# A two-layer vision tower on one core: first token weights from the unturned routing, weight loads split in six pieces, later weights rounded in small steps

## The chip, the core and the metric

The kernel runs on one core of one Trainium2 chip. Its engines are TensorE (PE in the profile; PEld is its weight load), VectorE (DVE), ScalarE (ACT), GpSimd (POOL) and SyncE (SP, which here only issues DMAs). Each runs its own list of instructions in order and waits on semaphores for the others. The metric is the time of one execution on the device in microseconds (us), the median of several; less is better. The profile is of one execution, with its own time.

## What is computed

Eight images of 256x256 become 8 x 64 patch tokens of 192 features, plus one class token each: 520 tokens. Then come attention 0, expert layer 0, attention 1 (with 8-bit fake quantisation) and expert layer 1, each after a layernorm and added to the running sum. The change touches the two expert layers, and the preparation of attention 1's weights:

```python
# expert layer 0: 8 experts of 768 hidden units, best 2 a token
router_probs = softmax(x @ w_gate);  top_p, top_i = top_k(router_probs, 2);  top_p /= sum(top_p)
h = gelu(x @ w_fc[expert]);  o = (h @ w_proj[expert]) weighted by top_p and summed
# expert layer 1: 16 experts of width 128 (8) and 256 (8), best 8 a token
probs = softmax(x @ router_w.T);  comb = normalised top-8 weights, zero elsewhere
out = sum over e of comb[:, e:e + 1] * (gelu(x @ w1[:, e]) @ w2[e])
# attention 1, weights (w_qkv and w_proj)
scale = max(max(abs(w), axis=1) / 127, 1e-8);  q = clip(round(w / scale), -128, 127);  w = q * scale
```

## The kernel before

The program is one block with a hand-written list for each engine. Tokens are kept as columns in the expert layers: 520 columns, in two halves of 260 (HALF). Every product there is made of parts rounded to a shorter format, hi and lo (x = hi + lo), so that three or more products of parts replace one in f32.

**ffn(y)** is expert layer y on each engine (PE L622 ff., ACT L1024 ff., DVE L1350 ff.). It runs over tiles of 128 hidden units: 48 in layer 0 (six an expert), 24 in layer 1. On PE, `entry("h", x)` makes the hidden units of tile x, five matmuls a half; `project(x)` multiplies them by the second weights and adds to the sums in banks 2 to 5 (SUMS), five matmuls a half (L601, L660). PE runs entry x + 2 ahead of project x. On ACT, `entry` reads the bank with gelu into hid, `hi_part(x)` rounds the weighted hidden units to hid_hi (L1043). On DVE, L1363 multiplies hid by the tile's token weights (128 equal rows, tok_w), and L1368 makes hid_lo. ENTRIES is the order in which entries take the two pairs of banks; an entry waits until ACT has emptied the bank of two entries before.

**Token weights.** `route` on DVE ends in comb, tokens by experts. `comb_turn` on PE turns it (L611) into banks 2 and 3, ACT copies it to comb_t (L1068, L1069), experts by tokens. For the first expert (MADE: turn 0 in layer 0, turns 0 and 1 in layer 1) `entry("w", turn)` multiplies comb_t by a one-hot matrix row_pick (L636) to get 128 equal rows, which ACT copies to tok_w (L1034). All later experts' rows are written by SP to DRAM (comb_to_dram) and read back to all partitions (token_weights, tok_w_in).

**Weights.** A load is one expert of layer 0 (2 x 768 columns of fc, 6 tiles x 192 of pj) or four tiles of layer 1; there are 8 + 6, in two slots. SP fetches it raw, when the split of the load two before is done (w_lo_done). While the tiles of load n run, load n + 1 is split: ACT copies a piece rounded (`weights_hi`, L1019, L1021), DVE subtracts (`weights_lo`, L1344, L1347). In before a load is three pieces, handled after the tiles j = 0, 1, 2 of the running load: fc part 0, fc part 1, pj. `next_weights(x)` stands on ACT after hi_part(x), and DVE's piece after hid_lo of tile x; each engine's next tile waits behind it.

**Later weights.** `whole_weights(piece)` on DVE prepares attention 1's eight rows of 192 x 96 weights: maxima, scale, reciprocal, product, rounding by adding and taking away MAGIC, clip. Its eight pieces stand after the tiles j = 3, 4, 5 of loads 0 to 2. `turn_weights` on PE turns them after ffn(0), and ACT copies them out (L1009 ff.).

`fill(n)` issues n matmuls of zeros. `then(...)` on DVE waits for the instruction's own completion, `settle(...)` only counts it.

## Time and profile before

| | us |
|---|---|
| median of 3 runs (lowest to highest) | 341.9 (341.59 to 342.23) |
| the profiled execution | 344.13 |
| its span, first to last instruction | 342.3 |
| PE busy (matmuls) | 290.1 |
| DVE busy | 258.6 |
| ACT busy | 207.2 |
| mean granted TensorE clock | 0.939 of full |

Expert layer 0 lasts from about 45.5 to 173, expert layer 1 from 269.8 to 333. So the two take more than half of the span. A busy share is an average over stages; what ends a wait last in a stage is read from the timelines, where `[0.63 <-ACT pj_parts L1021]` means that the engine was idle 0.63 us before this row and that ACT's instruction of line 1021 released it. Matmuls are pipelined: one of 260 columns shows 0.28 us, but the next starts 0.12 us after it.

### The profile page before, as it was taken

The page shows a single profiled execution, that of the slowest core. Times are in us where ns is not written, and L with a number is a line of the kernel's source. Part 1 is how long each engine was busy: PE and PEld are TensorE (multiplying, and loading weights), DVE is VectorE, ACT ScalarE, POOL GpSimd, SP SyncE. Part 2 cuts the span into 40 slices and gives each one's busy share as a digit, 9 for nine tenths or more (in the row PEclk, how much of TensorE's full clock was granted, in tenths as well). Part 3 has the DMA queues.
Part 4 walks back from the last instruction along what each step waited for, and adds up shares of the span by engine and source line. Part 5 has one row for each costly group of instructions (what it writes and reads, how often), then busy time and mean ns, then how long its engine had stood idle before and what let it go on. Part 6 is the DMA issues. An engine that isn't in the chain of part 4 may idle for free.

```text
span 342.3 us, 6186 instructions
## 1 busy us (share of the span) xinstructions
PE 290.1 (85%) x2351; PEld 263.4 (77%) x2351; DVE 258.6 (76%) x719; ACT 207.2 (61%) x489; POOL 14.2 (4%) x39
## 2 busy tenths in 40 slices
PE   8999989898989999999978307199877889999991
PEld 7979658898988999999967205068655479999991
DVE  1355767879888888889766899889858679888851
ACT  1063466575666867768738498687032777777750
POOL 0530000000000000000010001400000000000000
PEclk9999989999999999999999855589899999999997
DMA  7980016415050531200000000002400035542401
GB/s 249 317 265 1 2 19 234 166 33 190 5 192 2 192 113 53 107 3 0 2 0 2 0 2 2 0 0 67 149 3 0 0 99 171 159 156 90 96 0 47
DMA packets 10572, 27.28 MB, mean 80 GB/s; under 512 B 1368, under 2 KB 2216, under 8 KB 10544
## 3 DMA queue, kind: packets, MB, share of 16 engines
q1 hardware_dynamic: 10096, 26.20, 23.3%
q0 software_dynamic: 448, 0.70, 0.7%
q8 instruction: 18, 0.29, 0.4%
q14 instruction: 10, 0.08, 0.1%
HBM read 26.44 MB, written 0.45 MB: 79 GB/s over the span
## 4 chain that ended last, share of the span: by engine, by line
PE 50%; DVE 31%; ACT 12%; issue 4%; DMA 1%; DVEq 0%; ACTq 0%
PE bank L601 21%; PE bank L660 7%; PE bank L581 5%; ACT hid_hi L1043 4%; PE bank L699 4%; PE bank L645 3%; PE bank L643 3%; DVE hidden_area L1363 3%; DVE fc_lo L1344 2%; PE bank L571 2%; ACT fc_hi L1019 2%; DVE hid_lo L1368 2%; DVE pj_parts L1347 2%; ACT pj_parts L1021 1%; DVE bn L1264 1%
## 5 line engine op out<-in xcount | busy, mean ns | idle before, releaser
L1043 ACT ACTIVATE hid_hi<-hidden_area 128x260 fp32r<-128x260 f32 x144 | 55.6, 422 | 45.5 <-DVE hidden_area L1363 44.5
L601 PE MATMUL bank<-hid_hi,pj_parts 128*128 128x260 f32 x288 | 76.9, 288 | 4.9 <-DVE hid_lo L1368 4.9
L1368 DVE TENSOR_TENSOR hid_lo<-hidden_area,hid_hi 128x260 fp32r<-128x260 f32 x144 | 56.3, 427 | 10.1 <-ACT hid_hi L1043 1.1
L601 PEld LDWEIGHTS bank<-hid_hi,pj_parts 128*128 128x128 f32 x288 | 54.1, 188 | 6.7 <-DVE hid_lo L1368 6.0
L1036 ACT ACTIVATE hidden_area<-bank 128x260 f32<-128x260 f32 x144 | 48.3, 376 | 5.8 <-PE bank L645 5.3
L601 PE MATMUL bank<-xt_hi,fc_hi 128*128 128x260 f32 x144 | 41.9, 291 | 1.6 <-ACT hidden_area L1034 1.3
L645 PE MATMUL bank<-xt_lo,fc_lo 128*128 128x260 f32 x144 | 41.6, 289 | 0.0
L571 PE MATMUL bank<-zeros 128*128 128x260 bf16 x239 | 34.2, 296 | 8.6 <-ACT hidden_area L1175 6.7
L601 PE MATMUL bank<-xt_lo,fc_hi 128*128 128x260 f32 x144 | 40.9, 284 | 0.0
L643 PE MATMUL bank<-xt_lo,fc_hi 128*128 128x260 f32 x144 | 40.9, 284 | 0.0
L601 PE MATMUL bank<-xt_hi,fc_lo 128*128 128x260 f32 x144 | 40.8, 283 | 0.0
L660 PE MATMUL bank<-hid_hi,pj_parts 128*128 128x260 f32 x144 | 40.7, 283 | 0.0
L601 PE MATMUL bank<-hid_lo,pj_parts 128*128 128x260 f32 x144 | 40.7, 282 | 0.0
L660 PE MATMUL bank<-hid_lo,pj_parts 128*128 128x260 f32 x144 | 40.7, 282 | 0.0
L571 PEld LDWEIGHTS bank<-zeros 128*128 128x128 bf16 x239 | 23.9, 105 | 15.0 <-issue 8.3
L1363 DVE TENSOR_TENSOR hidden_area<-hidden_area 128x260 f32<-128x260 f32 x72 | 27.8, 423 | 7.0 <-ACT hidden_area L1034 6.2
L1363 DVE TENSOR_TENSOR hidden_area<-hidden_area,xn 128x260 f32<-128x260 f32 x72 | 28.0, 424 | 2.0 <-ACT hidden_area L1036 1.8
L1344 DVE TENSOR_TENSOR fc_lo<-raw_area,fc_hi 128x768 fp32r<-128x768 f32 (+1 forms) x28 | 23.6, 844 | 7.7 <-ACT fc_hi L1019 6.5
L601 PEld LDWEIGHTS bank<-xt_hi,fc_hi 128*128 128x128 f32 x144 | 27.4, 190 | 2.0 <-ACT hidden_area L1034 1.5
L601 PEld LDWEIGHTS bank<-xt_lo,fc_hi 128*128 128x128 f32 x144 | 27.4, 191 | 0.1
L601 PEld LDWEIGHTS bank<-xt_hi,fc_lo 128*128 128x128 f32 x144 | 27.4, 190 | 0.0
L645 PEld LDWEIGHTS bank<-xt_lo,fc_lo 128*128 128x128 f32 x144 | 27.3, 190 | 0.0
(296 smaller groups left out, 545.7 us busy)
## 6 DMA issues: line engine op xcount, KB each, us to landing
raw_area<-fc_dram SPq DMA_DIRECT2D x8, 768.0 KB, 4.4
raw_area<-pj_dram SPq DMA_DIRECT2D x8, 576.0 KB, 5.4
xn<-comb_dram SPq DMA_DIRECT2D x12, 260.0 KB, 3.2
raw_area<-fc_dram SPq DMA_DIRECT2D x6, 512.0 KB, 4.0
embed_area<-embed_in_dram SPq DMA_DIRECT2D x8, 352.0 KB, 6.1
hidden_area<-comb_dram SPq DMA_DIRECT2D x9, 260.0 KB, 3.2
raw_area<-pj_dram SPq DMA_DIRECT2D x6, 384.0 KB, 4.3
score_area<-w_l_dram SPq DMA_DIRECT2D x1, 576.0 KB, 8.9
```

What stands on the lines that cost most here:

```text
L571: pe.matmul(PB[bank][:, 0:HALF], zeros[:, 0:128], zeros[:], start=True, stop=True, skip_group_check=True)
L581: last = pe.matmul(out, lhs(kc), rhs(kc), start=(kc == 0), stop=(kc == KC - 1))
L601: mm = pe.matmul(out, lhs[a], rhs[b], start=start and n == 0, stop=stop and n == 2, skip_group_check=True)
L643: pe.matmul(out, fc_hi[:, s, 1, cols], x_mix[:, tok], start=False, stop=False, skip_group_check=True)
L645: mm = pe.matmul(out, fc_lo[:, s, 1, cols], x_mix[:, tok], start=False, stop=True, skip_group_check=True)
L660: mm = pe.matmul(PB[SUMS[2 + n]][:, 0:HALF], pj_tails[:, s, j], hidden[:, x % 3, tok], start=x == 0 and part == 0, stop=part == 1, skip_gr ...
L699: return pe.matmul(PB[i][:, 0:D], patches[:, k, i * 128:(i + 1) * 128], w_tok[:, k, :], start=(k == 0), stop=(k == TOKK - 1), skip_group_c ...
L1036: act.activation(hid[:, x % 2, tok], src, ACT.Gelu_apprx_tanh).then_inc(entry_out[y], 1)
L1043: act.activation(hid_hi[:, x % 3, tok], hid_w[:, x % 2, tok], ACT.Copy).then_inc(hid_hi_ready[y], 1)
L1344: dve.tensor_tensor(lo, raw, hi.bitcast(F32), ALU.subtract).then_inc(w_lo_done[s], 1)
L1363: dve.tensor_tensor(hid_w[:, x % 2, tok], hid[:, x % 2, tok], tok_w[tile.weights][:, tok], ALU.mult).then_inc(weighted[y], 1)
L1368: dve.tensor_tensor(hid_lo[:, x % 3, tok], hid_w[:, x % 2, tok], hid_hi[:, x % 3, tok].bitcast(F32), ALU.subtract).then_inc(hid_lo_ready[y ...
```

## The change

1. The first expert's token weights come from comb itself. `weights(out, turn, n)` multiplies a column of comb, repeated 128 times, by the identity, over the blocks of 128 tokens that a half touches: three matmuls a half. Turn 0 leaves ENTRIES, is written to banks 4 and 5, and ACT copies it (`first_weights`). comb_turn comes after it, and project(0) waits for comb_t_ready. Entry 1 comes right after entry 0, then five fills. In layer 1 turn 1 stands behind entry 2, not ahead of it. row_pick, its DMA, and the zeroing of comb_t go.
2. `pieces(load)`: six pieces for a load of layer 0 (four of fc with 384 columns, two of pj with three tiles), four for one of layer 1 (two of fc with 512, two of pj with two tiles), one after each of the first tiles. The pieces of load 0 are all made during attention 0.
3. `whole_weights` has 18 pieces after the tiles j = 0 to 3 of loads 1 to 4 and two of load 5 (WHOLE_AT). MAGIC is taken away by ACT when it copies the turned weights.

```diff
         for tiles in TILES:
-            order = [("h", 0), ("h", 1), ("w", 0)]
+            order = [("h", 0), ("h", 1)]
             for x in range(2, len(tiles)):
-                order += [("w", tiles[x].turn)] * (tiles[x].first and tiles[x].made) + [("h", x)]
+                order += [("h", x)] + [("w", tiles[x].turn)] * (tiles[x].first and tiles[x].made)
...
+        def pieces(load):
+
+            if LOAD_TILES[load] == T0:
+                return [("fc", 0, 0, 3), ("fc", 0, 3, 6), ("fc", 1, 0, 3), ("fc", 1, 3, 6), ("pj", None, 0, 3), ("pj", None, 3, 6)]
+            return [("fc", 0, 0, 4), ("fc", 1, 0, 4), ("pj", None, 0, 2), ("pj", None, 2, 4)]
...
+        WHOLE_AT = [(load, j) for load in range(1, 5) for j in range(4)] + [(5, 0), (5, 1)]
...
             def load0(n):
-                sp.wait_ge(w_lo_done[n % 2], 4 * (n // 2))
+                sp.wait_ge(w_lo_done[n % 2], split_lo(n - 2))
...
+                def weights(out, turn, n):
+
+                    e = tiles[first_tile(y, turn)].expert
+                    for i in (0, 1, 2) if n == 0 else (2, 3, 4):
+                        lo, hi = max(n * HALF, i * 128), min((n + 1) * HALF, i * 128 + rows(i))
+                        mm = pe.matmul(out[:, lo - n * HALF:hi - n * HALF],
+                                       (comb0, comb1)[y][0:rows(i), i, e:e + 1].broadcast_to([rows(i), 128]),
+                                       ident[0:rows(i), lo - i * 128:hi - i * 128], start=True, stop=True)
+                    return mm
...
                 def project(x):
                     s, j = tiles[x].slot, tiles[x].j
+                    if x == 0:
+                        pe.wait_ge(comb_t_ready, 2 * (y + 1))
...
                 entry("h", 0)
+                entry("h", 1)
+                fill(5, SUMS[0])
+                pe.wait_ge(comb_ready, y + 1)
+                for n in range(2):
+                    weights(PB[SUMS[2 + n]], 0, n).then_inc(first_w_mm, 1)
                 comb_turn(y, n_exp)
-                entry("h", 1)
-                pe.wait_ge(comb_t_ready, 2 * (y + 1))
-                entry("w", 0)
...
                     j, load = tiles[x].j, tiles[x].load
-                    if j <= 2 and load + 1 < LOADS:
-                        if j == 2 and load > E0 * y:
+                    if load + 1 < LOADS and j < len(pieces(load + 1)):
+                        if j == entry_pieces(load + 1) and load > E0 * y:
                             act.wait_ge(pj_mm[y], tiles_to(y, load - 1))
                         weights_hi(load + 1, j)
...
                 entry("h", 0)
+                first_weights()
+                hi_part(0)
                 comb_turned(y, (E0, E1)[y])
                 entry("h", 1)
-                entry("w", 0)
-                for x in range(len(tiles)):
-                    if x >= 2:
-                        for e in entries_of(y, x):
-                            entry(*e)
+                next_weights(0)
+                hi_part(1)
+                next_weights(1)
+                for x in range(2, len(tiles)):
+                    entry("h", x)
+                    if ("w", tiles[x].turn) in ENTRIES[y] and tiles[x].first:
+                        entry("w", tiles[x].turn)
                     hi_part(x)
                     next_weights(x)
...
+                    k = piece - 10
+                    then(dve.tensor_scalar(wq_int[:, k], wq_raw[:, k], wq_inv[:, k:k + 1], 127.0, ALU.mult, ALU.min))
+                    dve.tensor_scalar(wq_int[:, k], wq_int[:, k], -128.0, MAGIC, ALU.max, ALU.add).then_inc(wint_ready, 1)
```

How the instructions stand now at the places that the text below speaks of. PE at the start of ffn(0), before: after entry 0 the turning of comb (L611), entry 1, and the one-hot product (L636); comb is the routing, ident the identity.

```order
L645 MATMUL bank<-xt_lo,fc_lo 128x260
L611 MATMUL bank<-ident,comb 8x128 [waits comb_ready]
L611 MATMUL bank<-ident,comb 8x128 x3
L611 MATMUL bank<-ident,comb 8x8
L601 MATMUL bank<-xt_hi,fc_hi 128x260
```

The same place after, from the end of entry 1 on.

```order
L674 MATMUL bank<-xt_lo,fc_lo 128x260
L592 MATMUL bank<-zeros 128x260 x5
L652 MATMUL bank<-ident,comb 128x128 [waits comb_ready]
L652 MATMUL bank<-ident,comb 128x128
L652 MATMUL bank<-ident,comb 128x4
L652 MATMUL bank<-ident,comb 128x124
L652 MATMUL bank<-ident,comb 128x128
L652 MATMUL bank<-ident,comb 128x8
L632 MATMUL bank<-ident,comb 8x128 [waits comb_ready]
```

Entry 1 now stands ahead of all that waits for comb, and the turning behind the weights' product.

ACT at the same start, before (L1036 gelu, L1068 and L1069 the turned routing, L1034 the token weights, L1043 hid_hi):

```order
L1036 ACTIVATE hidden_area<-bank 128x260 [waits entry_mm0] x2
L1068 ACTIVATE comb_t<-bank 8x512 [waits comb_mm,comb_t_zero]
L1069 ACTIVATE comb_t<-bank 8x8
L1036 ACTIVATE hidden_area<-bank 128x260 [waits entry_mm0] x2
L1034 ACTIVATE hidden_area<-bank 128x260 [waits entry_mm0] x2
L1043 ACTIVATE hid_hi<-hidden_area 128x260 [waits weighted0] x2
L1019 ACTIVATE fc_hi<-raw_area 128x768 [waits raw_in1]
```

and after (L1071 gelu, L1092 the token weights, L1078 hid_hi, L1112 and L1113 the turned routing, L1054 a piece of fc):

```order
L1071 ACTIVATE hidden_area<-bank 128x260 [waits entry_mm0] x2
L1092 ACTIVATE hidden_area<-bank 128x260 [waits first_w_mm] x2
L1078 ACTIVATE hid_hi<-hidden_area 128x260 [waits weighted0] x2
L1112 ACTIVATE comb_t<-bank 8x512 [waits comb_mm]
L1113 ACTIVATE comb_t<-bank 8x8
L1071 ACTIVATE hidden_area<-bank 128x260 [waits entry_mm0] x2
L1054 ACTIVATE fc_hi<-raw_area 128x384 [waits raw_in1]
L1078 ACTIVATE hid_hi<-hidden_area 128x260 [waits weighted0] x2
```

The copies of the turned routing, the gelu of tile 1 and the first piece moved behind hid_hi of tile 0 and ahead of hid_hi of tile 1.

DVE around a tile of load 0, before (L1363 the weighting, L1368 hid_lo, L1344 and L1347 the pieces):

```order
L1363 TENSOR_TENSOR hidden_area<-hidden_area 128x260 [waits entry_out0] x2
L1368 TENSOR_TENSOR hid_lo<-hidden_area,hid_hi 128x260 [waits hid_hi_ready0] x2
L1347 TENSOR_TENSOR pj_parts<-raw_area,pj_parts 128x6x128 [waits w_hi_done1]
L1347 TENSOR_TENSOR pj_parts<-raw_area,pj_parts 128x6x64
L1363 TENSOR_TENSOR hidden_area<-hidden_area 128x260 [waits entry_out0] x2
```

and two tiles of load 4 after (L1412 the weighting, L1417 hid_lo, L1391 a piece, L1441 and L1442 a step of the later weights):

```order
L1412 TENSOR_TENSOR hidden_area<-hidden_area 128x260 [waits entry_out0] x2
L1417 TENSOR_TENSOR hid_lo<-hidden_area,hid_hi 128x260 [waits hid_hi_ready0] x2
L1391 TENSOR_TENSOR fc_lo<-raw_area,fc_hi 128x384 [waits w_hi_done1]
L1441 TENSOR_SCALAR score_area<-attn_area,wq_inv 96x192 [waits dve_done]
L1442 TENSOR_SCALAR score_area<-score_area 96x192 [waits dve_done]
L1412 TENSOR_TENSOR hidden_area<-hidden_area 128x260 [waits entry_out0] x2
```

Each tile of loads 0 to 6 now has a piece, half as large, and the tiles j = 0 to 3 a small step besides.

## Rows read from the trace of the kernel before

**Rows 1.** The page, chain that ended last: shares of the span by engine.

```profile
PE 50%; DVE 31%; ACT 12%; issue 4%; DMA 1%; DVEq 0%; ACTq 0%
```

**Rows 2.** Table by stretches: busy us of PE, PEld, DVE, ACT, POOL, granted clock, DMA.

```profile
49.00:50.00 1.00, 1.00 (x6) 1.00 (x6) 0.35 (x1) 0.64 (x2) 0.00 (x0) 0.50 0.00 0
...
120.00:130.00 10.00, 10.00 (x85) 10.00 (x84) 8.61 (x21) 6.96 (x20) 0.00 (x0) 1.00 0.38 140
```

**Rows 3.** Timeline of PE: start, us, instruction; project 2, 21, 22, 45; entry 3.

```profile
59.77 0.39 PE L601 MATMUL bank<-hid_hi,pj_parts 128*128 128x260 f32 x1 [0.19 <-DVE hid_lo L1368]
...
111.47 0.39 PE L601 MATMUL bank<-hid_hi,pj_parts 128*128 128x260 f32 x1 [1.04 <-DVE hid_lo L1368]
...
113.98 0.29 PE L601 MATMUL bank<-hid_hi,pj_parts 128*128 128x260 f32 x1
...
169.49 0.28 PE L601 MATMUL bank<-hid_hi,pj_parts 128*128 128x260 f32 x1
...
279.88 0.39 PE L601 MATMUL bank<-xt_hi,fc_hi 128*128 128x260 f32 x1 [1.29 <-ACT hidden_area L1034]
```

**Rows 4.** Timeline of DVE, tiles 1 to 4 of expert layer 0.

```profile
57.49 0.96 DVE L1344 TENSOR_TENSOR fc_lo<-raw_area,fc_hi 128x768 fp32r<-128x768 f32 x1 [0.30 <-ACT fc_hi L1019]
58.37 0.76 DVE L1363 TENSOR_TENSOR hidden_area<-hidden_area 128x260 f32<-128x260 f32 x2
...
60.68 1.43 DVE L1347 TENSOR_TENSOR pj_parts<-raw_area,pj_parts 128x768 fp32r<-128x768 f32 x2 [0.63 <-ACT pj_parts L1021]
62.02 0.76 DVE L1363 TENSOR_TENSOR hidden_area<-hidden_area 128x260 f32<-128x260 f32 x2
...
63.62 0.94 DVE L1385 TENSOR_REDUCE wq_amax<-attn_area 96x4 f32<-96x768 f32 x1
64.48 0.76 DVE L1363 TENSOR_TENSOR hidden_area<-hidden_area 128x260 f32<-128x260 f32 x2
```

**Rows 5.** Timeline of DVE, two tiles of load 4 without a piece.

```profile
125.93 0.76 DVE L1363 TENSOR_TENSOR hidden_area<-hidden_area 128x260 f32<-128x260 f32 x2
...
127.52 0.77 DVE L1363 TENSOR_TENSOR hidden_area<-hidden_area 128x260 f32<-128x260 f32 x2
```

**Rows 6.** Groups of ACT by form: busy us, mean ns of one, idle before.

```profile
L1019 ACT ACTIVATE fc_hi<-raw_area 128x768 fp32r<-128x768 f32 x16 | 13.3, 830 | 0.0
L1021 ACT ACTIVATE pj_parts<-raw_area 128x1152 fp32r<-128x1152 f32 x8 | 9.2, 1150 | 0.0
L1019 ACT ACTIVATE fc_hi<-raw_area 128x512 fp32r<-128x512 f32 x12 | 7.4, 616 | 0.0
```

**Rows 7.** Timeline of ACT, the pj piece after tile 2.

```profile
59.50 1.15 ACT L1021 ACTIVATE pj_parts<-raw_area 128x1152 fp32r<-128x1152 f32 x1
```

**Rows 8.** Timeline of DVE, attention 1: tensor_scalar of 1040 and 520 columns.

```profile
195.97 0.75 DVE L1525 TENSOR_SCALAR attn_area<-attn_area,consts 96x1040 f32<-96x1040 f32 x1
...
256.00 0.49 DVE L1525 TENSOR_SCALAR xn<-xn,consts 96x520 f32<-96x520 f32 x1
```

**Rows 9.** Timelines of ACT (first row) and PE at the starts, and small f32 matmuls.

```profile
49.12 0.59 ACT L1068 ACTIVATE comb_t<-bank 8x512 f32<-8x512 f32 x1 [0.40 <-PE bank L611]
...
48.06 0.96 PE L611 MATMUL bank<-ident,comb 128*8 128x128 f32 x5 [1.11 <-DVE comb L1335]
...
236.38 1.55 PE L876 MATMUL bank<-embed_area,attn_area 128*128 128x68 f32 x12
...
272.34 0.71 PE L611 MATMUL bank<-ident,comb 128*16 128x128 f32 x5 [1.12 <-DVE comb L1335]
...
274.27 1.92 PE L636 MATMUL bank<-comb_t,row_pick 128*128 128x260 f32 x8
275.84 0.47 PE L601 MATMUL bank<-xt_hi,fc_hi 128*128 128x260 f32 x1
```

**Rows 10.** Timeline of SP's queue, start of expert layer 1.

```profile
273.75 0.33 SPq L462 DMA_DIRECT2D comb_dram<-comb_t  x1
276.48 0.81 SPq L470 DMA_DIRECT2D xn<-comb_dram  x2
```

More of the change, by code:

```diff
@@ L426, in entries_of @@
             at = order.index(("h", x))
-            return order[at - 1:at + 1] if TILES[y][x].first and TILES[y][x].made else order[at:at + 1]
+            return order[at - 1:at + 1] if order[at - 1][0] == "w" else order[at:at + 1]
         def first_tile(y, turn):
@@ L634, in entry @@
                         if kind == "w":
-                            e = tiles[first_tile(y, x)].expert + (0, E0)[y]
-                            mm = pe.matmul(out, row_pick[:, e:e + 1].broadcast_to([128, 128]), comb_t[:, tok],
-                                           start=True, stop=True)
+                            mm = weights(out, x, n)
                         else:
@@ L1471, in _ @@
             dve.tensor_copy(ident_bf[:], ident[:]).then_inc(ident_ready, 1)
-            for piece in range(2):
+            for piece in range(4):
                 weights_lo(0, piece)
```

107 lines of the change are left out of this document (58 added, 49 removed).

## The prediction

> **What bounds the kernel now.** I read the views in this order: the chain that ended last by engine, the table by stretches, then the timeline of PE in the two expert stages (ffn, called for layer 0 and for layer 1), then the timelines of DVE and ACT in the same stretches. The chain gives PE half of the span, but DVE and ACT together 43% [rows 1]. The reason shows in ffn(0). From about 112 us on PE is busy without a hole and at full clock [rows 2], and a tile's round on it (one entry, one project, 20 matmuls) takes (169.49 - 113.98) / 23 = 2.4135 us; the two starts are the projects of tiles 22 and 45 [rows 3]. From tile 2 at 59.77 to tile 45 there are 43 rounds, which would need 103.78 us and took 109.72. So **5.94 us** are lost there, all before tile 22. The stall before tile 21 shows as 1.04 us in which PE waits for hid_lo [rows 3]; tiles 3, 9 and 15 have one like it. What comes last at that wait is DVE's queue.
>
> DVE's rounds, from one token-weight product (L1363) to the next, are these. A bare tile takes 127.52 - 125.93 = 1.59 [rows 5]. A tile with an fc piece of 768 columns takes about 2.8: 1.6 of its own, 0.88 for the piece (57.49 to 58.37), and 0.30 of waiting until ACT has rounded it [rows 4]. The pj tile takes 62.02 - 58.37 = 3.65, with 0.63 of waiting for ACT's 1.15 us copy [rows 4, 6]. A tile with a reduction of the later weights takes 64.48 - 62.02 = 2.46 [rows 4]. Three tiles of six with a load piece and three with a whole_weights piece are more than PE's 2.41 each time. After load 2 only the bare tiles are left beside the load pieces, and PE leads again.
>
> **Part 1, six pieces a load.** Take M as the start of a tile's product on DVE. ACT is through with hid_hi at M + 1.13 (59.50 against 58.37) [rows 4, 7], and PE's project can start at M + 1.40 (tile 2: 59.77 against 58.37) [rows 3, 4]. ACT's copy of 384 columns: 0.83 for 768 and 0.62 for 512 give 0.51 [rows 6]. DVE starts 0.03 after ACT ends (59.50 + 1.15 against 60.68) [rows 4, 7]. Its subtraction of 384 columns is 0.46: 1.34 for 768 and 384 together, less 0.88 for 768 [rows 4]. An **fc tile** is then 1.13 + 0.51 + 0.03 + 0.46 = 2.13. For a pj piece ACT takes 0.67 for 576 elements by the same line, and DVE 0.46 + 0.25 for 384 and 192: a **pj tile** is 1.13 + 0.67 + 0.03 + 0.71 = 2.54. A load is 4 x 2.13 + 2 x 2.54 = 13.60 against PE's 6 x 2.4135 = 14.48. The wait for DVE is mostly gone because each copy is short enough to lie under hid_lo. What is late next is DVE's own queue, by the small steps below. The pieces of load 0 move into attention 0, where ACT waits for s0 and DVE for o0 longer than a piece lasts; I cost them at nothing, and at most 0.3 if that cover is too thin. DVE's 1.4 us of pj subtraction after route goes; nothing waited for it but the SP queue.
>
> The Trainium skill (VectorE: DVE Perf Modes, the section on the TRN2 errata) says the opposite of this edit: each instruction pays a fixed latency of its own, so one should tile to 512 elements or more. By the Trainium skill's formulas, 58 cycles + elements at 0.96 GHz and 224 cycles + elements at 1.2 GHz, estimates are 0.46 us for DVE's 384 columns and 0.51 for ACT's, as the rows give; four more DVE instructions a load would be an estimate of 0.24 us, some 1.7 over seven loads, where DVE never waits.
>
> **Part 2, the later weights in small steps.** A reduction of 768 costs 2.46 - 1.59 = 0.87, one of 192 by DVE's 1.09 ns an element (0.88 - 0.46 over 384) 0.24. Loads 1 and 2 get four each. Scale and reciprocal stay small, 0.2 together, in load 3. Eight weights then take a pair of tensor_scalar of 192 columns with a wait for completion between them: two in load 3, four in load 4, two in load 5. That form at this width is not in the trace. From 0.75 us for 1040 and 0.49 for 520 columns [rows 8] one of 192 would last 0.33, and its successor would be issued 0.03 later and need 0.2: 0.56. If both issued back to back it would be 0.35. I take 0.5, near the first, since the wait is written out. The wait for pj_mm at piece 4 I put at 0.07 in loads 1 to 5.
> Against PE's 14.48, DVE's loads are: load 1 and 2 14.63 each; load 3 13.67 + 0.2 + 1.0 = 14.87; load 4 15.67; load 5 14.67. These exceed PE by 0.15, 0.15, 0.39, 1.19 and 0.19, **2.07 us** in sum.
>
> **Part 3, the start of each ffn.** Now: five transposes start at 48.06, when comb is ready, after 1.11 us in which PE idled [rows 9], and the granted clock is 0.50 from 49 to 50 [rows 2]: entry 1 runs at 1.2 GHz. After: entry 1 follows entry 0 at once (46.8 to 48.0), five fills end at 48.6, so PE has no hole before comb and I cost its work at the upper level. The Trainium skill (TensorE: Matmul & The Clock Gate, Part 1) calls the throttled level the default that activity releases; on that the new order should hold 2.4 GHz. The like hole before ffn(1), 1.12 us at 272.34 [rows 9], was followed by no such stretch, so the rule decides nothing there.
> The weights' product is six f32 matmuls where there were two. Two of 260 columns take 0.79 (four in the 1.57 us from 274.27 to 275.84) [rows 9]. One with 68 columns leaves 0.227 (236.38, twelve records for six matmuls, in 1.36) [rows 9]: weight loading sets it, so six take up to 6 x 0.23 = 1.36, and 0.79 at the least. I take 1.36, since the short ones are like the row. The first half's copy on ACT starts about 0.94 after its first matmul: 49.54. Then in ACT's queue: second copy, hid_hi twice (to 51.46), comb_turned 0.62 [rows 9] to 52.08, entry 1's gelu to 52.65, the first fc piece to 53.16. DVE must subtract that piece (to 53.65) before product 1, since it stands ahead of it. hid_hi 1, piece, gelu of tile 2 follow; product 2 starts at 55.77 and its hid_lo lets PE begin at 55.77 + 1.40 = 57.17. PE: project 0 at 52.2 (it now waits for comb_t_ready, as its banks hold the turned routing), project 1 at 55.05, **project 2 at 57.46** against 59.77. That is 2.31 earlier, and DVE leads by 0.29 there.
> For ffn(1) the same queue is: weights at 272.77 (comb is ready at 272.3 [rows 9]; entry 0 leaves PE near 271.05, ten matmuls and five fills follow), first copy 273.71, comb_turned to 276.25, entry 1's gelu to 276.82, fc piece of 512 columns to 277.44, its subtraction to 278.07, product 1, hid_hi 1, second piece, gelu of tile 2 from 279.72. Entry 3 on PE waits for that gelu's first half: 280.14, where it started at 279.88 [rows 3]. Now it waits for the second weights' copy, after for this gelu. So the time won at comb is given back: **0.26 us slower**, between 0.3 faster and 0.6 slower with the product's bounds. After it PE leads in both kernels.
> SP turns comb_t round some 2.3 us later relative to comb. In ffn(1) it was issued at 273.75 and the next issue came at 276.48 [rows 10]; moved by 2.6, token weights 2 would land near 282.5, tile 4 wants them near 284.5. In ffn(0) its first use is tile 6. The next loads' DMAs start up to three tiles later, with at least four tiles (9.6 us) before use against 5.4 us to land (the page's DMA issues). Both hidden.
>
> **The sum.** DVE leads by 0.29 at tile 2 and gains 4 x 2.41 - (2 x 2.13 + 2 x 2.54) = 0.31 in the rest of load 0: 0.60. The five loads then take 2.07, so PE stalls for 1.47. I add 0.3 for piece tiles at which DVE's lead is used up before the load's end and for the pair being nearer 0.56: 1.8. ffn(0) ends 2.31 + 5.94 - 1.8 = 6.45 earlier, ffn(1) takes 0.26 more, and all between is unchanged: 6.2 us. The profiled execution took 344.13 (1.8 of it outside its span of 342.3, untouched by the change), so 337.9 there; it lies 2.2 above the median of 341.9, on which the same saving gives **335.7**.
>
> **Rivals.**
> (a) DVE never binds: a pair costs 0.35, the product 0.79, or both. ffn(0) gains the whole 8.25 or a little more, ffn(1) is level: 333.6. For it: DVE's excess is small next to its lead. Against: the wait between the two steps of a pair.
> (b) DVE still paces ffn(0): each piece round costs 0.1 more than worked out (two semaphore waits ahead of a piece; ACT's gelu in between). Over the 34 piece rounds of loads 0 to 5 it adds 3.4: 339.1. For it: 2.13 and 2.54 rest on an ACT that starts each copy at once.
> (c) Slower: the handshake does not shrink with the piece, and DVE waits 0.30 at every fc piece and 0.63 at every pj piece as it does now. An fc tile is 2.36, a pj tile 2.93, a load 15.3, 1.7 more than above. Loads 0 to 6 then exceed PE by some 12 us, 10 more than in the forecast: 346. It decides from about 0.17 us more a round, where the 6.2 are used up over 36 rounds. Against: the present wait equals ACT's copy time less hid_lo to 0.03 us.
> (d) Slower by count of instructions: DVE busy time a load rises by 4 x 0.05 us for four more subtractions (0.46 - 384 x 1.09 ns each fixed), and by the pairs' 2.5 us, and PE follows DVE with no wait removed. That ends ffn(0) 1 to 2 us later: 343.5. It needs a DVE that never waits, and the rows with 0.30 and 0.63 speak against it. It is what the rule in the Trainium skill (VectorE: DVE Perf Modes, TRN2 errata) amounts to when taken alone.
> (e) The edits do not act: no wait of 1 us goes, as the last waited for is another. 341.9.
>
> **How the numbers follow.** Forecast 0.50, (a) 0.23, (b) 0.18, (c) 0.04, (d) 0.02, (e) 0.03. The range for 8 in 10 reaches from (a) with its bounds, 333.0, to just short of (b)'s end, 339.0. A measurement of this kernel tells about 0.2% (0.7 us) from no change. Faster: 0.50 + 0.23 + 0.18 = 0.91; same 0.03; slower 0.06.
>
> **What would show it.** PE's waits of 1 us for hid_lo in ffn(0) are gone, and small ones stand in loads 3 to 5, most in load 4. Tile rounds on DVE are near 2.13, 2.54, 2.37 with a reduction and 2.6 with a pair. Granted clock stays 1.00 from 45 to 53 us. Entry 3 of ffn(1) waits for ACT's gelu at about the same distance from comb as now. Wrong it would be if DVE's rounds are all above 2.41, if PE waits for raw weights or token weights from DMA, or if ffn(1) starts over 1 us later.

## The result, and the profile after

The changed kernel took **338.49 us** (median, 337.57 to 338.85, 4 runs) against 342.06 of the kernel before (341.59 to 344.02, 4 runs) on the same chip. The ratio is 0.9872, with a 95% interval of 0.9848 to 0.9897. In a second comparison it was 338.37 against 342.45, ratio 0.9883 [0.9861, 0.9905]. The forecast was 335.7 with a range of 333.0 to 339.0: the sign was right and the time lies in the range, but the saving was 3.6 to 4.1 us by the medians (4.0 to 4.4 by the ratios) where 6.2 were worked out. The profiled execution of the changed kernel took 338.60 us, its span is 336.7 and its mean granted clock 0.936.

The page of the changed kernel: busy time of the engines, and the chain that ended last. The second line answers [rows 1].

```profile
PE 292.5 (87%) x2385; PEld 265.4 (79%) x2385; DVE 263.4 (78%) x780; ACT 209.1 (62%) x519; POOL 13.7 (4%) x38
...
DVE 42%; PE 34%; ACT 16%; issue 5%; DMA 1%; DVEq 0%; ACTq 0%
```

DVE now holds the largest share of the chain: 42% where it had 31%, and PE 34% where it had 50%. So more of the program than before hangs on DVE. DVE itself is busy for 263.4 us in 780 instructions, where it was 258.6 in 719: the change gains by ending waits, as the rows below show, and pays with more work on the engine that had too much already.

Timeline of PE in the changed kernel: the start of project 2, the start of project 45, and the last matmul of ffn(0). The first two answer [rows 3].

```profile
57.27 0.29 PE L622 MATMUL bank<-hid_hi,pj_parts 128*128 128x260 f32 x1
...
163.43 0.28 PE L622 MATMUL bank<-hid_hi,pj_parts 128*128 128x260 f32 x1
...
167.30 0.28 PE L691 MATMUL bank<-hid_lo,pj_parts 128*128 128x260 f32 x1
```

From project 2 to project 45 it is 106.16 us, 2.38 more than the 43 rounds of 2.4135; before it was 5.94 more. Project 45 and the two behind it follow each other without entries between them. The last matmul comes 3.87 us after project 45 starts, where it came 3.48 after it before. That is 0.39 more, and the sum had no term for it. The whole stage from project 2 on thus exceeds its bound by 2.77 us instead of 5.94.

Timeline of DVE in the changed kernel: two fc tiles and two pj tiles of load 0, a tile with a reduction, a tile with a pair. It answers [rows 4].

```profile
55.02 0.56 DVE L1391 TENSOR_TENSOR fc_lo<-raw_area,fc_hi 128x384 fp32r<-128x384 f32 x1
55.50 0.76 DVE L1412 TENSOR_TENSOR hidden_area<-hidden_area 128x260 f32<-128x260 f32 x2
...
57.16 0.56 DVE L1391 TENSOR_TENSOR fc_lo<-raw_area,fc_hi 128x384 fp32r<-128x384 f32 x1
57.64 0.76 DVE L1412 TENSOR_TENSOR hidden_area<-hidden_area 128x260 f32<-128x260 f32 x2
...
62.34 0.76 DVE L1412 TENSOR_TENSOR hidden_area<-hidden_area 128x260 f32<-128x260 f32 x2
...
64.17 0.83 DVE L1394 TENSOR_TENSOR pj_parts<-raw_area,pj_parts 128x384 fp32r<-128x384 f32 x2
64.92 0.76 DVE L1412 TENSOR_TENSOR hidden_area<-hidden_area 128x260 f32<-128x260 f32 x2
...
67.06 0.34 DVE L1433 TENSOR_REDUCE wq_amax<-attn_area 96x1 f32<-96x192 f32 x1
67.32 0.41 DVE L1412 TENSOR_TENSOR hidden_area<-hidden_area 128x260 f32<-128x260 f32 x1
...
101.07 0.31 DVE L1441 TENSOR_SCALAR score_area<-attn_area,wq_inv 96x192 f32<-96x192 f32 x1
101.41 0.26 DVE L1442 TENSOR_SCALAR score_area<-score_area 96x192 f32<-96x192 f32 x1
101.58 0.76 DVE L1412 TENSOR_TENSOR hidden_area<-hidden_area,xn 128x260 f32<-128x260 f32 x2
```

The waits in brackets of [rows 4], 0.30 at an fc piece and 0.63 at a pj piece, are gone from these rows. The largest wait for a piece between here and the end of ffn(0) is 0.22, at the first pj piece after the tiles of loads 1 to 6. A round, from product to product, is 2.14 with an fc piece (57.64 - 55.50), 2.58 with a pj piece (64.92 - 62.34), 2.40 with a reduction (67.32 - 64.92), and a pair adds 0.51 (101.58 - 101.07).

Timelines of the changed kernel at the start of ffn(0), DVE, PE, ACT and DVE again, and in the last row entry 3 of ffn(1) on PE. They answer [rows 9] and the last of [rows 3].

```profile
47.63 0.20 DVE L1381 TENSOR_TENSOR comb<-comb,rinv 128x40 f32<-128x40 f32 x1
...
47.80 0.73 PE L592 MATMUL bank<-zeros 128*128 128x260 bf16 x5
48.37 1.59 PE L652 MATMUL bank<-ident,comb 128*128 128x128 f32 x12
49.89 0.70 PE L632 MATMUL bank<-ident,comb 128*8 128x128 f32 x5
...
49.13 0.39 ACT L1092 ACTIVATE hidden_area<-bank 128x260 f32<-128x260 f32 x1 [0.59 <-PE bank L652]
50.00 0.39 ACT L1092 ACTIVATE hidden_area<-bank 128x260 f32<-128x260 f32 x1 [0.47 <-PE bank L652]
...
51.81 0.63 ACT L1071 ACTIVATE hidden_area<-bank 128x260 f32<-128x260 f32 x2
52.34 0.51 ACT L1054 ACTIVATE fc_hi<-raw_area 128x384 fp32r<-128x384 f32 x1
...
52.88 0.56 DVE L1391 TENSOR_TENSOR fc_lo<-raw_area,fc_hi 128x384 fp32r<-128x384 f32 x1 [1.05 <-ACT fc_hi L1054]
53.36 0.76 DVE L1412 TENSOR_TENSOR hidden_area<-hidden_area 128x260 f32<-128x260 f32 x2
...
274.30 0.39 PE L622 MATMUL bank<-xt_hi,fc_hi 128*128 128x260 f32 x1 [0.81 <-ACT hidden_area L1071]
```

DVE has finished comb at 47.83, but PE first runs its five fills and starts the weights' product at 48.37. ACT copies the weights, then has six more instructions before the first fc piece, and DVE waits 1.05 us for that piece before product 1. The end of the last comb instruction (L1381, here 47.83) is the point from which I measure below.

### The profile page after: what moved, and what is told of

Same layout as the page of the kernel before. It is cut to its first block, busy times and chain, and to the rows that moved or that the text cites. A ratio compares the mean times of both kernels' runs of the same rounds, so it can differ in the third digit from the quotient of the medians.

```text
span 336.7 us, 6345 instructions
## 1 busy us (share of the span) xinstructions
PE 292.5 (87%) x2385; PEld 265.4 (79%) x2385; DVE 263.4 (78%) x780; ACT 209.1 (62%) x519; POOL 13.7 (4%) x38
## 4 chain that ended last, share of the span: by engine, by line
DVE 42%; PE 34%; ACT 16%; issue 5%; DMA 1%; DVEq 0%; ACTq 0%
PE bank L622 11%; ACT hid_hi L1078 7%; DVE hid_lo L1417 7%; DVE hidden_area L1412 5%; DVE fc_lo L1391 5%; PE bank L602 5%; PE bank L732 4%; DVE pj_parts L1394 3%; PE bank L691 3%; ACT pj_parts L1056 3%; PE bank L592 2%; PE bank L674 2%; PE bank L672 2%; DVE bn L1310 1%; DVE score_area L1702 1%
## 5 line engine op out<-in xcount | busy, mean ns | idle before, releaser
L1078 ACT ACTIVATE hid_hi<-hidden_area 128x260 fp32r<-128x260 f32 x144 | 55.6, 422 | 39.3 <-DVE hidden_area L1412 38.3
L1417 DVE TENSOR_TENSOR hid_lo<-hidden_area,hid_hi 128x260 fp32r<-128x260 f32 x144 | 56.3, 427 | 10.3 <-ACT hid_hi L1078 1.5
L1071 ACT ACTIVATE hidden_area<-bank 128x260 f32<-128x260 f32 x144 | 48.0, 375 | 4.1 <-PE bank L674 3.8
L592 PE MATMUL bank<-zeros 128*128 128x260 bf16 x249 | 36.5, 301 | 8.2 <-ACT hidden_area L1221 6.4
L622 PE MATMUL bank<-xt_hi,fc_hi 128*128 128x260 f32 x144 | 41.2, 286 | 1.1 <-ACT hidden_area L1071 0.8
L592 PEld LDWEIGHTS bank<-zeros 128*128 128x128 bf16 x249 | 25.0, 106 | 15.5 <-issue 8.2
L1412 DVE TENSOR_TENSOR hidden_area<-hidden_area 128x260 f32<-128x260 f32 x72 | 27.9, 423 | 5.4 <-ACT hidden_area L1092 4.4
L1391 DVE TENSOR_TENSOR fc_lo<-raw_area,fc_hi 128x384 fp32r<-128x384 f32 (+1 forms) x44 | 26.0, 595 | 5.2 <-ACT fc_hi L1054 4.1
L1412 DVE TENSOR_TENSOR hidden_area<-hidden_area,xn 128x260 f32<-128x260 f32 x72 | 27.7, 422 | 1.3 <-ACT hidden_area L1071 1.1
L622 PEld LDWEIGHTS bank<-hid_lo,pj_parts 128*128 128x128 f32 x144 | 27.3, 190 | 0.0
```

The source lines that it names most:

```text
L592: pe.matmul(PB[bank][:, 0:HALF], zeros[:, 0:128], zeros[:], start=True, stop=True, skip_group_check=True)
L622: mm = pe.matmul(out, lhs[a], rhs[b], start=start and n == 0, stop=stop and n == 2, skip_group_check=True)
L1071: act.activation(hid[:, x % 2, tok], src, ACT.Gelu_apprx_tanh).then_inc(entry_out[y], 1)
L1078: act.activation(hid_hi[:, x % 3, tok], hid_w[:, x % 2, tok], ACT.Copy).then_inc(hid_hi_ready[y], 1)
L1391: dve.tensor_tensor(lo, raw, hi.bitcast(F32), ALU.subtract).then_inc(w_lo_done[s], 1)
L1412: dve.tensor_tensor(hid_w[:, x % 2, tok], hid[:, x % 2, tok], tok_w[tile.weights][:, tok], ALU.mult).then_inc(weighted[y], 1)
```

## Which ruler to use

Three stretches make up ffn(0) as DVE sees it: from the end of comb to product 1, from product 1 to product 47, and from there to PE's last matmul. They are read from the timelines of DVE and PE of each kernel; for the changed one 53.36 - 47.83, 164.72 - 53.36 and 167.30 - 164.72. The column for ffn(1) is the time from the end of its comb to the start of project 21, the last that has an entry in front.

| kernel | comb to product 1 | product 1 to 47 | 47 to last matmul | sum | ffn(1) |
|---|---|---|---|---|---|
| before, first profile | 7.50 | 114.00 | 3.46 | 124.96 | 57.16 |
| before_again | 6.01 | 113.99 | 3.46 | 123.46 | 57.17 |
| first_only | 6.26 | 114.36 | 3.46 | 124.08 | 57.40 |
| pieces_only | 5.31 | 111.14 | 3.47 | 119.92 | 57.18 |
| old_start | 5.30 | 111.45 | 2.57 | 119.32 | 57.17 |
| old_steps | 5.53 | 111.15 | 3.47 | 120.15 | 57.42 |
| after | 5.53 | 111.36 | 2.58 | 119.47 | 57.39 |
| after_again | 5.54 | 111.36 | 2.58 | 119.48 | 57.41 |
| gelu_early | 4.99 | 111.40 | 2.56 | 118.95 | 56.87 |
| late_steps | 5.53 | 110.88 | 2.57 | 118.98 | 57.41 |
| all_three | 4.61 | 110.88 | 2.58 | 118.07 | 56.49 |
| mid_steps | 5.51 | 110.38 | 2.57 | 118.46 | 57.39 |
| mid_old_start | 5.28 | 110.36 | 2.57 | 118.21 | 57.17 |
| mid_early | 4.62 | 110.36 | 2.58 | 117.56 | 56.48 |

Where the same code runs, the numbers repeat to 0.05 us or so. The rest of the program does not: comb of layer 0 is complete anywhere from 46.86 to 48.12 us, and from the last matmul of ffn(0) to comb of layer 1 it takes 99.01 to 99.63, with and without any part of the change. One profiled span alone could therefore not have told the parts apart; these distances can. Where a text below says "by the table", before_again is the kernel before.

## Experiments

**before_again and after_again: both kernels once more, unchanged, side by side on one chip.**

> The kernel before, profiled once more. In the two profiles the span fell by 5.6 us (342.3 to 336.7), in the medians by 3.6 (342.06 to 338.49). Theory H (the hole's clock): the first profile of before caught entry 1 of expert layer 0 at 1.2 GHz (granted clock 0.50 from 49 to 51.6 us), which most executions do not have; then this profile shows 1.00 there, starts project 0 about 1 us sooner after comb, and its span is near 340.4. Theory F (a fixed part): every execution of before has that stretch; then the clock is 0.50 again at the same place and the span is near 342, and the medians differ for a reason that lies elsewhere (attention 1, whose clock is 0.50 for some 25 us in both).

> The changed kernel, timed in five rounds against before to have the size of the change. By the medians 3.6 us faster, by the two profiled spans 5.6. Theory H says 3.5 to 4.5, theory F 5.5. The trace should show the same 2.4 us lost between project 2 and project 45 of expert layer 0, all from tile 19 to 34.

before_again took 342.62 us with a span of 340.8, 1.5 less than the 342.3 of the first profiled execution; after_again took 338.37 with a span of 336.6. Table by stretches and timelines of before_again (PE, DVE, PE):

```profile
49.00:50.00 1.00, 1.00 (x11) 1.00 (x10) 0.34 (x1) 0.89 (x3) 0.00 (x0) 1.00 0.00 0
...
48.06 0.70 PE L611 MATMUL bank<-ident,comb 128*8 128x128 f32 x5 [1.12 <-DVE comb L1335]
...
47.81 0.20 DVE L1335 TENSOR_TENSOR comb<-comb,rinv 128x40 f32<-128x40 f32 x1
...
58.28 0.39 PE L601 MATMUL bank<-hid_hi,pj_parts 128*128 128x260 f32 x1 [0.20 <-DVE hid_lo L1368]
```

The transposes start at the same 48.06 behind the same hole (1.12 against 1.11 in [rows 9]). But the granted clock of 49:50 is 1.00 here and 0.50 in [rows 2], PE gets eleven matmuls into that microsecond instead of six, and project 2 starts at 58.28 instead of 59.77. So 1.49 us of the 2.31 that the prediction gave to the new start were a stretch at 1.2 GHz that this execution of the same program does not have. Nor has any other: the granted clock is 1.00 from 46 to 54 us in all thirteen other profiles, four of which (before_again, pieces_only, old_start, mid_old_start) have the old start with its hole. The median of before (342.45) sits at before_again's time, not at the first profile's.

**first_only: part 3 alone.** Three large pieces a load and the eight large rounding steps are put back.

```diff
 def pieces(load):
-    if LOAD_TILES[load] == T0:
-        return [("fc", 0, 0, 3), ("fc", 0, 3, 6), ... ("pj", None, 3, 6)]
-    return [("fc", 0, 0, 4), ... ("pj", None, 2, 4)]
+    w = LOAD_TILES[load]
+    return [("fc", 0, 0, w), ("fc", 1, 0, w), ("pj", None, 0, w)]
...
+WHOLE_AT = [(load, j) for load in range(3) for j in (3, 4, 5)][:8]
```

> Only the start of each expert layer changed (token weights from comb, entry 1 first); three pieces a load and the later weights' eight large steps as before. Theory R (DVE's rounds are what is saved): project 2 comes some 1.3 us earlier in expert layer 0 where before has the 1.2 GHz stretch, 0.3 where it has not; the waits of 1 us for hid_lo stay, so that 6 us are lost again between project 2 and project 45; expert layer 1 is 0.3 slower. In sum between level and 1 us faster. Rival S (the start is what is saved): 3 us or more faster.

Measured 343.44 (342.7 to 343.88, 12 runs), ratio 1.0021 [1.0005, 1.0036]: a little slower than before. In the table it needs 0.25 more to product 1, 0.37 more to product 47 and 0.23 more in ffn(1), 0.85 in sum, and the medians give 0.99. I had expected it level to 1 us faster, with project 2 coming 0.3 earlier; it comes 10.50 us after comb where before_again has it at 10.27. The 0.37 is nearly all in one place: before the pj piece of load 2's tiles DVE waits 1.05 us for ACT (at 91.78), where it waits 0.70 in before_again. Part 3 has no gain of its own.

**old_start: parts 1 and 2 without part 3.** PE's part of the edit; ACT's order, the order of entries and row_pick go back with it.

```diff
 entry("h", 0)
-entry("h", 1)
-fill(5, SUMS[0])
-pe.wait_ge(comb_ready, y + 1)
-for n in range(2):
-    weights(PB[SUMS[2 + n]], 0, n).then_inc(first_w_mm, 1)
 comb_turn(y, n_exp)
+entry("h", 1)
+pe.wait_ge(comb_t_ready, 2 * (y + 1))
+entry("w", 0)
```

> Six pieces a load and small steps of the later weights, but the start of each expert layer as before. Theory R: rounds of 2.14, 2.57, 2.39 and 2.66 us on DVE, some 2.0 us lost between project 2 and 45 in place of 6, project 2 about 0.9 us earlier than before since the first piece ahead of product 1 is half as large; expert layer 1 level with before. In sum 4.5 to 5 us faster than before, within 1 us of the whole change and perhaps faster than it. Rival S: under 1.5 us faster.

Measured 338.12 (337.96 to 339.22, 6 runs), ratio 0.9875 [0.9854, 0.9896]: the same as the changed kernel beside it (0.9883), whose interval it overlaps almost wholly. By the table it is 0.15 ahead in ffn(0) and 0.22 in ffn(1). The whole gain of the change is parts 1 and 2.

**pieces_only: part 1 alone** (old_start, and the eight large steps as in first_only).

> Part 1 alone: six pieces a load, the rounding in the eight large steps of before, the old start. Theory S: the stall from project 2 to project 45 goes from 5.9 us (before) to that of old_steps, 3.4 to 3.5; nothing else moves, so the median is 2.5 us under that of before, near 340.0 (ratio 0.993). If instead the smaller pieces cost VectorE the fixed part of twice as many instructions without hiding a wait (rival b of the prediction), the stall stays over 4.5 us and the gain is under 1.5 us.

Measured 339.43 (338.88 to 339.75, 4 runs), ratio 0.99 [0.9872, 0.9928]. By the table 0.70 is won up to product 1 and 2.85 up to product 47, 3.54 in sum with the last column; the medians give 3.2. I had expected 2.5, with a stall up to project 45 of 3.4 to 3.5 and nothing else moved; the stall is 3.21, and the 0.70 before product 1 was not in that sum. So the smaller pieces are most of the change. Timeline of DVE in pieces_only, end of comb and product 1:

```profile
47.69 0.20 DVE L1380 TENSOR_TENSOR comb<-comb,rinv 128x40 f32<-128x40 f32 x1
...
53.20 0.76 DVE L1409 TENSOR_TENSOR hidden_area<-hidden_area 128x260 f32<-128x260 f32 x2
```

5.31 us with the old start, where the changed kernel with its new start needs 5.53. The share of [rows 3] that I had put down to the start came from the pieces: the first fc piece stands ahead of product 1 on DVE in every one of these kernels, and it is now half as long on both engines. A gain under 1.5 us, expected here if the smaller pieces only cost DVE more fixed parts, is out with it.

**old_steps: parts 1 and 3, the eight large steps of before.**

> The changed kernel with the later weights' eight large steps as before (after tiles j = 3, 4, 5 of loads 0 to 2), pieces and start as changed. Theory R adds DVE's rounds: tiles of load 0 to 2 with a large step last 2.14 + 0.87 or 2.57 + 0.87; the three loads exceed PE's 14.48 by 1.0, 1.1 and 1.0, less a lead of 0.3: 2.8 us lost between project 2 and 45 against 2.4 in the changed kernel. So 0.4 us slower than the changed kernel. Rival P (small steps are what removed the long waits): waits of 1 us return and it is 2 us or more slower.

Measured 339.22 (338.2 to 339.74, 6 runs), ratio 0.9898 [0.9874, 0.9923], which is 0.5 to 0.9 us over the changed kernel's two ratios. The table has it 0.68 over the changed kernel in ffn(0), and pieces_only 0.60 over old_start. Part 2 is thus worth 0.6 to 0.7 us. I had expected 0.4, so the direction held and the size was low.

**late_steps: the small steps spread over all loads.** The theory was that the stall of 2.4 us comes from too many steps in loads 3 to 5.

```diff
-WHOLE_AT = [(load, j) for load in range(1, 5) for j in range(4)] + [(5, 0), (5, 1)]
+WHOLE_AT = [(1, 0), (1, 1), (1, 2), (2, 0), (2, 1), (2, 2), (3, 0), (3, 1), (3, 2), (3, 3),
+            (4, 0), (5, 0), (6, 0), (6, 2), (7, 2), (7, 3), (7, 4), (7, 5)]
```

> The changed kernel with the 18 small steps spread otherwise: three reductions each after the first tiles of loads 1 and 2, two in load 3, and the eight pairs one each in loads 4 and 5, two in load 6 and four in load 7, where DVE's load pieces are small. No load then takes DVE much over PE's 14.48. Theory R: the 2.4 us lost in tiles 19 to 34 fall to 0.3 or less, so about 2.1 us faster than the changed kernel. Rival Q (the loss is PE's wait for something else, such as hid_hi's buffers or DMA): no change.

Measured 338.19 (337.3 to 340.3, 6 runs), ratio 0.9876 [0.9842, 0.9909]: no more than the changed kernel, where 2.1 us had been expected. The stall up to project 45 did vanish: that project starts at 160.85, exactly 43 rounds behind project 2. But the time came back within the next two tiles. Timelines of late_steps, DVE and then PE:

```profile
163.56 0.31 DVE L1442 TENSOR_SCALAR score_area<-attn_area,wq_inv 96x192 f32<-96x192 f32 x1
163.90 0.26 DVE L1443 TENSOR_SCALAR score_area<-score_area 96x192 f32<-96x192 f32 x1
164.08 0.76 DVE L1413 TENSOR_TENSOR hidden_area<-hidden_area,xn 128x260 f32<-128x260 f32 x2
...
167.04 0.76 DVE L1449 COPY xt<-bank 128x260 f32<-128x260 f32 x2 [0.77 <-PE bank L692]
...
163.36 0.39 PE L623 MATMUL bank<-hid_hi,pj_parts 128*128 128x260 f32 x1 [1.13 <-DVE hid_lo L1418]
165.47 0.39 PE L623 MATMUL bank<-hid_hi,pj_parts 128*128 128x260 f32 x1 [0.65 <-DVE hid_lo L1418]
```

PE waits 1.13 and 0.65 us for hid_lo ahead of its last two projects. So the missing stall up to project 45 saved nothing: PE reached its last projects earlier and then waited there for DVE.

**gelu_early: ACT takes entry 1's gelu ahead of the copies of the weights.**

```diff
 entry("h", 0)
+entry("h", 1)
 first_weights()
 hi_part(0)
 comb_turned(y, (E0, E1)[y])
-entry("h", 1)
 next_weights(0)
```

> The changed kernel with one line moved on ACT: the gelu of tile 1 stands before the copy of the first token weights, where ACT waits 0.59 us for the product anyway, instead of behind the copy of the turned routing. Theory C (ACT's queue is the chain at the start): product 1 on DVE, and all that follows it, comes 0.55 us earlier in both expert layers: 1.0 us faster in all, since DVE's lag carries through expert layer 0 and PE's wait for the gelu of tile 2 in layer 1 shrinks by as much. Rival: the chain there is PE or the product of the weights, no change.

Measured 338.21 (337.42 to 338.28, 5 runs), ratio 0.9866 [0.9841, 0.9891]. The table shows the expected 1 us nearly whole: 0.54 less to product 1 (4.99 against 5.53) and 0.52 less in ffn(1). The ratio is lower than the changed kernel's by 0.0006 to 0.0017, which the intervals don't tell from nothing or from the 0.0031 that 1.05 us would be. The theory stands by the distances alone here, and by mid_early below.

**all_three: late_steps, gelu_early and no fills ahead of the weights' product.**

> Late steps, early gelu and no fills between entry 1 and the weights' product. If the three terms add: 2.1 + 1.0 + 0.4 to 0.9 (the fills hold the product back by 0.45 us after comb in each layer), 3.5 to 4 us faster than the changed kernel, some 334.7. If the clock falls for want of the fills, the stretch after comb shows 0.50 and 1 to 2 us of that go.

Measured 336.86 (335.4 to 338.86, 6 runs), ratio 0.9829 [0.9796, 0.9862], where 334.7 had been expected; what is missing is the 2.1 us of late_steps. Against gelu_early the fills' absence gives 0.38 up to product 1 and 0.38 in ffn(1).

**mid_steps: two pairs behind the last tile.** My theory for late_steps was that two of its pairs stood badly, just ahead of the last tiles.

```diff
+WHOLE_AT = [(1, 0), (1, 1), (1, 2), (2, 0), (2, 1), (2, 2), (3, 0), (3, 1), (3, 2), (3, 3),
+            (4, 0), (5, 0), (6, 0), (6, 2), (7, 2), (7, 4), (7, 5), (7, 5)]
```

> The changed kernel with only the table of the rounding steps altered: the eight reductions stay in loads 1 to 3, but the eight pairs now stand in (4,0), (5,0), (6,0), (6,2), (7,2), (7,4) and two behind the last tile (7,5). Against late_steps the pairs of (7,3) and the earlier half of the last tiles' work are gone. Theory E (the end): late_steps lost what it had gained because its pairs in tiles 45 and 46 made VectorE late for tiles 46 and 47. Then project 45 starts near 160.9 (0 to 0.2 us of stall from tile 2), the copy of the sums comes 3.9 to 4.1 us behind it instead of 6.2, about 2.2 us earlier than in the changed kernel, and the median is 2.0 to 2.4 us under the changed kernel's, near 336.2. Rival G (given back): whatever is gained inside ffn(0) is lost behind it, for example by the clock or by a wait for the rounded weights; then the median stays within 0.5 us of 338.2.

Measured 337.53 (337.14 to 338.12, 5 runs), ratio 0.9848 [0.9819, 0.9876]: 0.8 to 1.2 us better than the changed kernel by the ratios, and neither the 2.0 to 2.4 of theory E nor the nothing of rival G. The copy of the sums comes 5.65 us behind project 45 (166.25 - 160.60), where theory E wanted 3.9 to 4.1. Timelines of mid_steps, DVE and PE:

```profile
163.29 0.76 DVE L1413 TENSOR_TENSOR hidden_area<-hidden_area,xn 128x260 f32<-128x260 f32 x2
...
166.25 0.77 DVE L1450 COPY xt<-bank 128x260 f32<-128x260 f32 x2 [0.25 <-PE bank L692]
...
162.57 0.39 PE L623 MATMUL bank<-hid_hi,pj_parts 128*128 128x260 f32 x1 [0.60 <-DVE hid_lo L1418]
164.68 0.39 PE L623 MATMUL bank<-hid_hi,pj_parts 128*128 128x260 f32 x1 [0.65 <-DVE hid_lo L1418]
```

Both tables together settle it. From product 1 to product 47 the changed kernel takes 111.36 with all eight pairs between them; late_steps, which has one pair behind product 47, takes 110.88; mid_steps, which has two there, 110.38. The differences are 0.48 and 0.98: one and two times the 0.51 of a pair. Where among the tiles the other pairs stand makes no difference that shows. The busy time of DVE says the same. Tables by stretches of before_again, the changed kernel and mid_steps, each from product 1 to product 47 (busy us of PE, PEld, DVE, ACT, POOL, granted clock, DMA):

```profile
54.02:168.01 113.99, 109.44 (x891) 107.83 (x891) 97.36 (x225) 79.92 (x206) 0.00 (x0) 1.00 0.25 87
...
53.36:164.72 111.36, 111.23 (x902) 109.13 (x901) 101.57 (x273) 81.28 (x229) 0.00 (x0) 1.00 0.25 88
...
52.91:163.29 110.38, 109.66 (x907) 109.24 (x906) 100.65 (x268) 81.46 (x229) 0.00 (x0) 1.00 0.25 89
```

DVE is not busy for 16.63 us in before_again, for 9.79 in the changed kernel and for 9.73 in mid_steps. The last two differ in what DVE has to do, not in what it waits. So with the small steps ffn(0) runs at the pace of DVE's queue from product 1 to product 47; only work that leaves the queue or a wait that ends inside it counts. In the changed kernel DVE waits 1.29 us for PE before it copies the sums, as the timeline of its DVE shows:

```profile
167.69 0.76 DVE L1448 COPY xt<-bank 128x260 f32<-128x260 f32 x2 [1.29 <-PE bank L691]
```

With the two pairs there it waits 0.25, so this place is full.

**mid_old_start: the same table with the old start.**

> The same table of steps, six pieces a load, but the old start of both feed-forward stages (the turned routing, the weights as third entry). Theory F: part 3 of the change brings nothing to an ordinary execution, so this kernel's median is within 0.5 us of mid_steps, about 336.2. Theory H as first predicted (part 3 is worth some us at project 2): it would be 1 to 2 us slower than mid_steps.

Measured 336.95 (336.26 to 337.31, 4 runs), ratio 0.9827 [0.9799, 0.9855]: 0.6 us below mid_steps by the medians and 0.7 by the ratios, where theory F had within 0.5 and theory H 1 to 2 us above it. Theory H is out; the 336.2 expected was missed as in mid_steps. The table gives it 0.25 less in ffn(0) and 0.22 less in ffn(1).

**mid_early: mid_steps with gelu_early and without the fills.**

```diff
-fill(5, SUMS[0])
...
 entry("h", 0)
+entry("h", 1)
 first_weights()
```

> mid_steps, and ScalarE takes the gelu of entry 1 ahead of the copies of the first weights, and no fillers before the weights' product. all_three was 1.3 us under late_steps by the medians and 2.7 by the profiled spans; the same edits on the better table should give the same: 334.9, range 334.2 to 335.6. Theory Q (ScalarE's queue order at the start costs nothing): within 0.4 us of mid_steps.

Measured **335.93** (334.94 to 336.44, 5 runs), ratio 0.9797 [0.977, 0.9823], the fastest here and under both kernels of this case; 334.9 had been expected, in a range of 334.2 to 335.6. The miss comes from mid_steps, which itself came out 1.3 above what was expected of it. It is 1.6 below mid_steps, for which the table has 0.90 in ffn(0) and 0.91 in ffn(1). Timelines of mid_early at the start of ffn(0), PE and ACT, and a row of its table by stretches:

```profile
47.74 1.69 PE L653 MATMUL bank<-ident,comb 128*128 128x128 f32 x12
...
47.73 1.23 ACT L1071 ACTIVATE hidden_area<-bank 128x260 f32<-128x260 f32 x4
48.81 0.42 ACT L1092 ACTIVATE hidden_area<-bank 128x260 f32<-128x260 f32 x1
49.47 0.39 ACT L1092 ACTIVATE hidden_area<-bank 128x260 f32<-128x260 f32 x1 [0.23 <-PE bank L653]
...
48.00:49.00 1.00, 1.00 (x10) 0.93 (x9) 0.00 (x0) 1.00 (x5) 0.00 (x0) 1.00 0.00 0
```

The product starts 0.06 us after comb is complete instead of 0.54, both gelus lie under PE's work, and the second copy of the weights ends at 49.86, 2.18 after comb (47.68), where it was 2.56 in the changed kernel (50.39 - 47.83). The granted clock is 1.00 without the fills too. So the new start does pay, once the fills and the gelu are out of its way. By this start as a whole ffn(0) and ffn(1) are 0.65 and 0.69 faster than with the old one (mid_early against mid_old_start), and by the ratios 1.0 us. How much of that is the product from the unturned routing, and how much entry 1 and its gelu standing ahead, no run parts: an old start with entry 1 moved ahead was not tried.

## Why the prediction was right, and where it was off

**What bounds the kernel: right, and not carried far enough.** DVE's queue cost ffn(0) 5.94 us before, and it paces the stage in the changed kernel. But I balanced DVE against PE load by load and counted what exceeded PE's 14.48, as if PE could be ahead again afterwards.

**Part 1, the rounds: right.** 2.13 for an fc tile measured 2.14; 2.54 for a pj tile measured 2.57 and 2.58. A load without steps is 13.78 instead of 13.60 (load 6, products 36 to 42: 140.09 to 153.87), because its first pj tile takes 2.63, with the wait at piece 4 that I had put at 0.07. That wait shows as 0.22 us in which DVE has ACT's pj piece still to come. The fixed cost per instruction that the Trainium skill (VectorE: DVE Perf Modes, TRN2 errata) warns of is there: a piece of 768 took 0.88 from start to start [rows 4], and its two halves take 0.48 each (55.50 - 55.02), 0.08 more together. But the waits removed are worth more here: part 1 alone is 3.5 us by the table. That the pieces of load 0 are hidden held: comb of layer 0 is complete at 47.89 in pieces_only and at 48.01 in before_again. That the DMAs are hidden held too: no wait of an engine in either expert layer of the changed kernel is ended by a DMA.

**Part 2: right in kind, low in size.** The reduction's round was 2.40 for 2.37, the pair 0.51 for 0.5. With the pj tiles of above the loads 1 to 5 take 14.79, 14.80, 14.93, 15.83 and 14.82. That exceeds PE by 2.77 us in sum, where 2.07 was worked out: errors of mostly 0.01 to 0.03 a tile, nearly all in the same direction, over 30 tiles. The stall up to project 45 was 2.38 for 1.8.

**The end of ffn(0): missing from the sum.** Three projects stand without an entry between them at the end, so PE needs a tile every 1.21 us there, and DVE, with 1.6 of its own a tile, can't follow unless it is ahead. Before it was ahead, as its last five loads had no steps. Now it is not: 0.39 us. The runs part it by the steps: from product 47 to the last matmul it is 3.46 or 3.47 in every kernel with the eight large steps and 2.56 to 2.58 in every one with the small ones, so with these DVE is late to the end.

**Part 3, the start: right in its steps, wrong in what it was credited with.** Product 1 was forecast at 53.65 and came at 53.36, project 2 at 57.46 and came at 57.27; the queue followed instruction by instruction held. But the working took all 2.31 us as the fruit of the new order. The runs split it: 1.49 were the stretch at 1.2 GHz in the one profiled execution, 0.83 was part 1 (project 2 comes 10.27 after comb in before_again, 9.45 in pieces_only and 9.44 in after), and part 3 itself nothing. Of the small terms, the six small matmuls took 1.52 us (48.37 to 49.89) where 1.36 was taken, and the fills hold PE 0.49 us past the time at which it could have had comb (comb complete at 47.83, the product at 48.37, 0.05 being the usual distance).

**ffn(1): right.** 0.26 us slower was forecast. In the table it is 57.39 to 57.42 with the new start and ACT's old order, 57.16 to 57.18 with the old start: 0.23. Entry 3 waits for ACT's gelu as described, 7.82 us after comb is complete where it was 7.60.

**The sum.** On the profiled executions 5.6 us were saved (342.3 to 336.7) of 6.2. Term by term: 2.32 at project 2 (2.31 forecast), 3.17 from there to the end of ffn(0) (4.14), 0.23 lost in ffn(1) (0.26), and 0.34 won in the two attention stages and the rest, which is within what these vary by anyway. The step that failed for the time itself is the last: "the same saving" was taken off the median. That the time still lies in the range is owed to an upper end that was set for rival (b), whose mechanism did not come. The saving held 1.49 us that only the profiled execution had to give, and its excess of 2.2 over the median was there to warn of it. Without it the forecast would have been 4.7 saved, 337.2; with the measured stall and the end of ffn(0) 3.7, which is 338.2 on 341.9.

**Rivals.** (a), that DVE never binds, is out: the pair cost 0.51 and the product 1.52. (b) came near in time (339.1) but not in mechanism: the rounds of loads 1 to 5 were about 0.02 over in the mean, not 0.1. (c) is out, since no wait of 0.30 or 0.63 is left, and (d), since the removed waits did bring time. (e) is out: part 1 alone gives 3.2 to 3.5 us.

**What stays open.** The two attention stages vary by up to 1.3 and 0.6 us between profiled executions. I made no experiment on that, and don't know why. What made the clock fall in one of fourteen profiled executions is open too. Nor did I try to move work out of DVE's queue onto POOL, which is busy 4%.

## What to carry to other kernels

When one engine's queue feeds another all through a stage, only work taken out of that queue, or waits ended inside it, shorten the stage; moving its work about inside moves the stall and not the end, so look for the idle stretch behind the last product and fill it. Halve a handed-over piece when the wait for the first engine's copy is longer than what the second can do meanwhile. And before the saving is taken from one profiled execution, ask which of its stretches the median doesn't have: an execution 2 us over its median may carry something that no edit will earn.
